# An attention and FFN block on one core: prelude re-ordered, a cast one slot later, eight banks for the last outputs, maxima 8 slots ahead instead of 10

## What is computed

```python
xn = layernorm(X)
Q, K, V = xn @ W_q.T, xn @ W_k.T, xn @ W_v.T          # 16 heads of 16
Qr, Kr = rope(Q), rope(K)
scores = einsum('bhqd,bhkd->bhqk', Qr, Kr) * 16 ** -0.5  # causal
heads = einsum('bhqk,bhkd->bhqd', softmax(scores), V)
attn = heads.reshape(b, t, d) @ W_o.T
ffn = fake_quant_fp8(xn) @ fake_quant_fp8(weight).T + bias   # one scale per tensor
out = X + attn + ffn
```

## Time and profile before

| | us |
|---|---|
| median of 3 runs | 456.89 |
| range of the runs | 455.64 to 457.11 |
| the profiled execution | 456.14 |
| its span in the trace | 454.2 |

### The profile page before, as it was taken

The page is one execution under the profiler, slowest core; times in us unless marked ns, Lnnn a source line. Parts: engine busy times, 40 slices in busy tenths (PEclk is TensorE's granted clock), DMA queues, the critical chain, the costliest instruction groups (busy, mean ns, idle before and its releaser), DMA issues.

```text
span 454.2 us, 9406 instructions
## 1 busy us (share of the span) xinstructions
PE 400.0 (88%) x2911; PEld 234.7 (52%) x2911; DVE 353.9 (78%) x1372; ACT 278.6 (61%) x505; POOL 284.4 (63%) x284
## 2 busy tenths in 40 slices
PE   7906769987889999999999999999999999899866
PEld 7505434443545645564556555655556555464434
DVE  2996778999797978987898869887988698779213
ACT  2664757565763766576756676576667666667631
POOL 2675674468577678667866866778668764245740
PEclk9966898999999999999999999999999999999999
DMA  8859226633267058714762366525762477020111
GB/s 273 270 162 218 39 71 156 132 65 118 84 126 141 2 164 193 136 25 137 198 138 45 116 184 123 92 74 176 138 129 71 149 156 143 2 93 3 49 46 46
DMA packets 34049, 53.16 MB, mean 117 GB/s; under 512 B 4496, under 2 KB 30480, under 8 KB 31120
## 3 DMA queue, kind: packets, MB, share of 16 engines
q1 hardware_dynamic: 34000, 52.57, 46.9%
HBM read 35.52 MB, written 16.78 MB: 115 GB/s over the span
## 4 chain that ended last, share of the span: by engine, by line
PE 45%; DVE 18%; issue 12%; POOL 9%; ACT 9%; DMA 5%; SPq 1%; POOLq 0%; DVEq 0%; ACTq 0%
PE o_ps L931 10%; PE st_ps L844 9%; DVE scratch L600 8%; PE s_ps L864 7%; PE m_ps L829 6%; ACT prob L712 5%; PE m_ps L896 4%; PE m_ps L873 4%; POOL rot L308 3%; POOL rot L300 2%; POOL rot L301 2%; DMA xnT<-x_dram 2%; DMA q_st<-shift 1%; POOL parts L313 1%; POOL prob L458 1%
## 5 line engine op out<-in xcount | busy, mean ns | idle before, releaser
L600 DVE CUSTOM_DVE_ANT_0 scratch<-s_ps,causal 128x512 bf16<-128x512 f32 (+3 forms) x512 | 220.5, 484 | 48.3 <-PE s_ps L864 48.1
L712 ACT ACTIVATE prob<-st_ps 128x512 f32<-128x512 f32 x320 | 174.5, 600 | 103.5 <-PE st_ps L844 102.4
L458 POOL TENSOR_SCALAR_AFFINE_SELECT prob<-prob 128x512 f32<-128x512 f32 (+1 forms) x160 | 92.1, 579 | 127.3 <-ACT prob L712 126.6
L864 PE MATMUL s_ps<-k_st,q_st 96*128 96x512 bf16 (+3 forms) x512 | 122.3, 301 | 24.1 <-DMA k_st<-qk_parts 14.5
L844 PE MATMUL st_ps<-q_st,k_st 98*128 98x128 bf16 (+3 forms) x512 | 122.5, 302 | 15.1 <-ACT prob L712 11.2
L844 PEld LDWEIGHTS st_ps<-q_st,k_st 98*128 98x128 bf16 x512 | 41.2, 97 | 97.5 <-ACT prob L712 57.9
L931 PE MATMUL o_ps<-prob,v_sb 128*17 128x512 f32 (+3 forms) x1024 | 81.4, 435 | 2.3 <-POOL prob L458 1.8
L864 PEld LDWEIGHTS s_ps<-k_st,q_st 96*128 96x128 bf16 x512 | 48.5, 98 | 47.9 <-DVE rowmax L600 17.4
L600 DVE DVE_READ_ACCUMULATOR2_ANT rowmax<- 128x1 f32 x512 | 41.2, 80 | 0.0
L931 PEld LDWEIGHTS o_ps<-prob,v_sb 128*17 128x17 f32 x1024 | 23.0, 96 | 31.0 <-issue 24.4
L313 POOL TENSOR_TENSOR parts<-rot,parts 128x1024 bf16<-128x1024 f32 (+1 forms) x16 | 32.7, 2046 | 2.3 <-ACT parts L698 2.3
(11 more groups left out here) (101 smaller groups left out, 519.1 us busy)
## 6 DMA issues: line engine op xcount, KB each, us to landing
qk_parts<-parts SPq DMA_DIRECT2D x16, 768.0 KB, 3.7
q_st<-qk_parts SPq DMA_DIRECT2D x15, 384.0 KB, 4.9
k_st<-qk_parts SPq DMA_DIRECT2D x15, 384.0 KB, 7.2
xnT<-x_dram SPq DMA_DIRECT2D x8, 512.0 KB, 8.8
q_st<-qk_parts SPq DMA_DIRECT2D x15, 256.0 KB, 3.8
k_st<-qk_parts SPq DMA_DIRECT2D x15, 256.0 KB, 8.3
x_res<-x_dram SPq DMA_DIRECT2D x7, 512.0 KB, 3.5
out_dram<-x_res SPq DMA_DIRECT2D x7, 512.0 KB, 2.9
```

The costliest lines, as they stand in the source:

```text
L458: eng.affine_select(out=ap, in_=ap, compare_op=ALU.is_ge, fill=0.0, base=0, pattern=pat, channel_multiplier=-1).then_inc(masked, 1)
L600: eng.tensor_tensor_reduce(scratch[:, at % 3, col:col + w], s_ps[at % 3][:, col:col + w], causal[:, T - w:T], 1.0, NEG, ALU.add, ALU.max, ...
L712: eng.activation(prob[u][:, half * T:(half + 1) * T], st_ps[ST_BANK[2 * s + half]][:, :], ACT.Exp, scale=SCALE).then_inc(exp_done, 1)
L864: mm = eng.matmul(bank[:, col:col + (qb + 1) * P], q_st[0:ROWS, n % 2, h, qb * P:(qb + 1) * P], k_st[0:ROWS, n % 2, h, 0:(qb + 1) * P], st ...
```

## The change

- **Lead.** `LEAD` 10 to 8. The maxima, and with them "mt" of groups 0 and 1 (one slot later), the first slot, and the slots in which batches 3 to 7 are turned, follow. The second item of V comes one slot earlier.
- **Chain.** The offsets are now tables. The `middle` cast of the keys moves from -21 to -20, their write from -19 to -18. Batch 1 has slots of its own (`EARLY`, `EARLY_CHAIN`), some of them after slot 0.
- **Prelude.** Batch 1's x is loaded ahead of cos and sin; both fills of `k_st` come ahead of the second `invert`; DVE does all of batch 0's remainders and lows; the weights' casts come first on ACT, their splits come early on POOL; `statistics` of batches 6 and 7 move into slots -8 and -6; batch 0's parts are written part by part (`write_first`), two writes more for each of queries and keys; the dummy products go from 26 and 8 to 22 and 6, and 46 new ones fill PE's wait, tied to the last low cast and to the last write.
- **End.** For the last batch "o", "at" and "fin" leave the schedule. Behind it four banks take the turned heads and the outputs, four others the turned `attn`, with four buffers for its copy. The products of the input go in ahead of those of attention. In slot 160 the attention products of blocks 1 and 3 wait for four masks only, and block 2 alone waits for the fifth.

The core of the diff:

```diff
-LEAD = 10
+LEAD = 8
-OFFSETS = {("v", 0): 0, ("mt", 1): 1, ("v", 1): 2, ("o", 0): 23, ("o", 1): 24, ("o", 2): 25, ("o", 3): 26, ("mt", 2): 7,
+OFFSETS = {("v", 0): 0, ("v", 1): 1, ("mt", 1): 2, ("o", 0): 23, ("o", 1): 24, ("o", 2): 25, ("o", 3): 26, ("mt", 2): 7,
            ("at", 0): 28, ("qk", 0): -32, ("at", 1): 29, ("qk", 1): -30, ("fin", 0): 31, ("at", 2): 32, ("mt", 3): 12,
-           ("qk", 2): -27, ("fin", 1): 34, ("at", 3): 34, ("qk", 3): -25, ("fin", 2): 36, ("mt", 0): -4, ("fin", 3): 38}
+           ("qk", 2): -27, ("fin", 1): 34, ("at", 3): 34, ("qk", 3): -25, ("fin", 2): 36, ("mt", 0): -3, ("fin", 3): 38}
-TURN_SLOT = {3: -10, 4: -9, 5: -7, 6: -5, 7: -3}
+EARLY = {("qk", 0): -6, ("qk", 1): -5, ("qk", 2): -4, ("qk", 3): -3}
+CHAIN = {("rotate", 0): -29, ("high", 0): -28, ("remainder", 0): -27, ("middle", 0): -26, ("low", 0): -25,
+         ("write", 0): -24, ("rotate", 1): -24, ("high", 1): -23, ("remainder", 1): -22, ("middle", 1): -20,
+         ("low", 1): -19, ("write", 1): -18, ("read", 0, 0): -18, ("read", 0, 1): -16, ("read", 1, 0): -12,
+         ("read", 1, 1): -11}
+EARLY_CHAIN = {("rotate", 0): -4, ("high", 0): -4, ("remainder", 0): -3, ("middle", 0): -3, ("low", 0): -2,
+               ("write", 0): -1, ("rotate", 1): -1, ("high", 1): -1, ("remainder", 1): 0, ("middle", 1): 2,
+               ("low", 1): 3, ("write", 1): 4, ("read", 0, 0): -1, ("read", 0, 1): 6, ("read", 1, 0): 8,
+               ("read", 1, 1): 9}
+TURN_SLOT = {3: -LEAD, 4: -LEAD + 1, 5: -LEAD + 2, 6: -LEAD + 4, 7: -LEAD + 6}
...
+            def write_first(w):
+                for t, (done, out_) in enumerate(((hi_done, early_out), (mid_done, early_out), (low_done, parts_out))):
+                    eng.wait_ge(done[w], 2)
+                    eng.dma_start(qk_dram[0, w].rearrange("t r j h n -> (j h) t r n")[:, t],
+                                  parts[:, w, t]).then_inc(out_[w], 16)
...
-            for n in range(4):
+            for n in range(3):
                 statistics(n)
-            eng.wait_ge(w_qk_in, 16 * 4)
+            eng.wait_ge(cos_in, 16 * 2)
             rope(0, 0, first_ps[0])
             rope(0, 1, first_ps[1])
             rotate(eng, 0, 0)
             rope(0, 2, first_ps[2])
+            remainder(eng, 0, 0)
             rope(0, 3, first_ps[3])
             rotate(eng, 0, 1)
+            low(eng, 0, 0)
             remainder(eng, 0, 1)
             low(eng, 0, 1)
-            for n in range(4, NB):
+            for n in range(3, 6):
                 statistics(n)
...
-            keep_busy(26)
+            keep_busy(22)
             turn_rows(0)
-            keep_busy(8)
+            keep_busy(6)
             for k in range(4):
                 project_whole(k)
             turn_rows(1)
             turn_rows(2)
+            keep_busy(20)
+            eng.wait_ge(low_done[1], 2)
+            keep_busy(16)
+            eng.wait_ge(parts_out[1], 16)
+            keep_busy(10)
...
+            last = NB - 1
+            eng.wait_ge(max_done, ITEMS * NB)
+            eng.wait_ge(fin_done, 4 * last)
+            for qb in range(NQ):
+                turn_heads(last, qb, tail_o[qb]).then_inc(full["o"], 1)
+            eng.wait_ge(exp_done, HALVES * NB)
+            for qb in range(NQ):
+                turn_attn(last, qb, tail_at[qb]).then_inc(full["at"], 1)
+                if qb > 0:
+                    output_of_attn(last, qb - 1, tail_o[qb - 1], False).then_inc(full["fin"], 1)
+                output_of_input(last, qb, tail_o[qb], True)
+            output_of_attn(last, NQ - 1, tail_o[NQ - 1], False).then_inc(full["fin"], 1)
```

More of the change, by code:

```diff
@@ L214, in attention_ffn_block @@
         first_ps = m_ps + s_ps[0:2]
+        tail_o, tail_at = s_ps + m_ps[0:1], m_ps[1:2] + st_ps + [o_ps]
         turn_ps = (st_ps[0], o_ps)
@@ L223, in attention_ffn_block @@
         parts_out = [sem(f"parts_out{w}") for w in range(2)]
+        early_out = [sem(f"early_out{w}") for w in range(2)]
         first_in = [sem(f"first_in{g}") for g in range(2)]
@@ L461, in _ @@
             nw = NC * D
-            for n in range(3):
-                invert(n)
-            eng.wait_ge(ln_rstd, 6)
+            eng.wait_ge(consts, 6)
             fill_ones(0)
             eng.wait_ge(consts, 7)
-            remainder(eng, 0, 0)
-            low(eng, 0, 0)
+            invert(0)
+            eng.wait_ge(ln_rstd, 2)
+            fill_ones(1)
+            eng.wait_ge(consts, 8)
+            invert(1)
+            eng.wait_ge(ln_rstd, 4)
             split_weights(0)
+            eng.wait_ge(w_split, 1)
+            invert(2)
+            eng.wait_ge(ln_rstd, 6)
             split_weights(1)
+            eng.wait_ge(w_split, 2)
+            eng.memset(v_sb[:, :, :, :], 1.0).then_inc(consts, 1)
+            eng.wait_ge(consts, 9)
+            eng.wait_ge(low_done[1], 2)
+            invert(3)
+            invert(4)
             split_x(1)
-            for n in range(3, 6):
-                invert(n)
-            eng.memset(v_sb[:, :, :, :], 1.0).then_inc(consts, 1)
-            eng.wait_ge(consts, 8)
+            invert(5)
             for slot in range(FIRST_SLOT, END_SLOT):
@@ L658, in _ @@
                     row_max(n, 2 * s + 1)
+                if slot in (-LEAD, -LEAD + 2):
+                    statistics({-LEAD: 6, -LEAD + 2: 7}[slot])
                 if slot in range(1, 2 * NB, 2):
@@ L671, in _ @@
                        .then_inc(qc_done, 1)
+            for qb in range(NQ):
+                norm(NB - 1, qb, tail_o[qb])
+            for qb in range(NQ):
+                finish(NB - 1, qb, tail_o[qb])
         @block.scalar
@@ L735, in _ @@
             normalise(0)
+            eng.wait_ge(w_qk_in, 16 * 2)
+            for parts_of, raw in zip(w_parts, (wq_sb, wk_sb)):
+                eng.copy(parts_of[:, 0], raw).then_inc(w_high, 1)
             copy_turned(0)
@@ L788, in _ @@
                         copy_heads(n, g)
-                for off, step, w in ((-28, high, 0), (-26, middle, 0), (-23, high, 1), (-21, middle, 1)):
-                    n = batch_at(slot, off, 1)
+                for name, step, w in (("high", high, 0), ("middle", middle, 0), ("high", high, 1), ("middle", middle, 1)):
+                    n = chain_at(slot, name, w)
                     if n is not None:
                         step(n, w)
+            for qb in range(NQ):
+                copy_at(NB - 1, qb, tail_at[qb])
         @block.tensor
```

121 lines of the change are left out of this document (76 added, 45 removed).

## The result

The changed kernel takes 460.54 us (median of 8 runs, 459.67 to 463.02), the kernel before 457.0 on the same chip (8 runs, 453.6 to 458.12): ratio 1.0098, 95% interval 1.0062 to 1.0134. The forecast was 442.8 with a range of 439.0 to 449.0. The profiled run of the change took 459.71, its span is 458.0 against 454.2.

The account below looks back on a forecast made before the run. PE was taken to bound the middle batches and DVE batch 0. Prelude -8.5, middle -3.3, shifts +1.4, last-batch maxima +1.0 and end -4.7 sum to -14.1, from 456.89 to 442.8 us; range 439 to 449.

Parts of the forecast that it names:

- The path to the first slot, -3.0: Prelude: last low cast 1.7 us and keys' write 1.3 us sooner, so PE's maxima start at 35.2 instead of 38.21.
- The rule by which more transfers would cost 4 us: Prelude writes in thirds: at about 2.0 us fixed cost each, two more starts add 4 us, sum -10.1; a rival.
- The slots ahead of batch 0, -7.7: Eight slots before batch 0: first exponential at 59.8 instead of 67.54, a gain of 7.7 us lasting until slot 20.
- In batch 0 DVE is the bound and covers both: Batch 0: no cost there from later shifts of groups 0 and 1, because DVE bounds that batch.
- The check by parts (3.0, 3.5 and 1.0): First exponential's 7.7 us gain: 3.0 from the start, 3.5 from the `k_st` fill, 1.0 from the cast ahead of it.
- The clock term of 0.8: PE's clock of 0.8 from 68 to 79 us, after the late exponential, improves; 0.8 us taken between 0 and 2.3.
- The middle, -3.3: Batches 1 to 6: later cast removes a 0.71 us wait each, 4.3; earlier V projection loses 0.15 each time.
- The shifts, +1.4: Shorter lead makes group 0's shifts for slot 20 late by 0.2 us in each of 7 batches.
- The shifts come late in every batch: Rival, 8%: group 0's shifts 1.0 us late per batch instead of 0.2, giving 448.4 us.
- Slower: Rival, 3%: shift landings of 4.6 us make groups 0 and 1 late, 3.5 us in 7 batches, giving 466.
- Two slots of maxima in the last batch, +1.0: Two slots' worth of maxima products move into the last batch's second half, partly covered by PE's waits; costs 1.0 us.
- the end, -4.7: After the last batch: `heads` copy 1.0 us sooner, turns without a reader between; last finish begins 446.9 instead of 451.55.

Follow-up runs that it names:

- run 5: Changed kernel with one number back: SP issues the keys' write in slot -19 instead of -18, all other lists unchanged; 448.85 us, ratio 0.9854.
- run 4: Kernel before with only the keys' middle cast, low cast and write a slot later (-20, -19, -18); 448.44 us, ratio 0.9831.
- run 9: Run 5 with the second V projection back in slot 2, behind the turn of group 1's maxima; 446.34 us, ratio 0.9811.
- run 11: Kernel before with the new end alone; lead, prelude and casts as before; 451.43 us, ratio 0.9912.
- run 12: Kernel before with the late cast and the new end together, old prelude and lead of 10; 444.46 us, ratio 0.9757.
- run 7: Changed kernel with lead 9, batch 1's chain mended and group 1's turn in slot 1 (443.22 us), keys' write put back from -19 to -18; 442.37 us.
- run 6: Run 4 with the second V projection moved to slot 1 and the turn of group 1's maxima to slot 2; 472.09 us, ratio 1.0352.
- run 8: Changed kernel with the shift pairs issued from ACT's queue instead of SP's, SP keeping its wait for the shift; 521.45 us, ratio 1.1442.

## Why the forecast failed, step by step

Two steps failed: the shifts of group 2 behind the late write (11.7 us), and what the earlier start is worth (some 3.5 us). With the write's one number mended (run 5) the time is 448.85, still 6 us above the 442.8. In the spans, run 5 against the kernel before: 5.0 gained ahead of the first landmark where 8.5 were forecast, 1.4 in the middle where 1.9 were, 3.4 behind it where 3.7 were. (Its trace is of its fastest execution: the spans differ by 9.8, the medians on its chip by 6.7.)

**The path to the first slot, -3.0: right.** PE's first maxima came 4.1 us sooner than in the trace before. That trace has a late start: the old prelude's first maxima lie between 37.02 and 38.21 in four traces, the new one's between 33.97 and 34.58 in all, so some 3 us are the change's. The rule by which more transfers would cost 4 us did not decide. By the Trainium skill, DMA: Bandwidth & Descriptors (Rules for kernel authors), the sum was to be -10.1, an estimate; no such loss at the start shows in the rows.

**The slots ahead of batch 0, -7.7: right in the row, wrong in what it is worth.** The first exponential came 6.7 sooner, at 60.87 against the forecast 59.8. The step that failed is "As DVE waits only at the start of batch 0, a gain there lasts until slot 20". The landmark in slot 23 gained 3.4 of it (5.0 in run 5). DVE is the bound of batch 0, so its list had to be summed, not the way to ACT's first exponential. Its first maxima come 3.8 to 4.8 us sooner (35.51 against 39.34 to 40.33 with the old prelude) and have 4.2 us of `statistics` behind them that stood ahead before; and it waits for PE's scores for 8.8 us between 55 and 118, where it waited 3.9 before, as PE stands for the shifts of groups 0 and 2 (1.92 at 57.40, 2.66 at 81.82). "In batch 0 DVE is the bound and covers both" is wrong for the same reason: DVE's maxima need PE's products, and these stand behind the stalled scores on PE. The check by parts (3.0, 3.5 and 1.0) was mis-sized too: the cast alone is worth over 3 of it (run 4), not 1.0. The clock term of 0.8 has no run of its own; ahead of the first landmark the clock rose from 0.90 to 0.96, but behind the two waits just named it was near 0.86 (57 to 69 us and 80 to 92 us), so part of it was lost again.

**The middle, -3.3: right about the cast, and too small.** The 0.71 waits are gone, and run 4 has the cast by itself: 7.5 us. In its trace 5.4 lie between the landmarks, where 4.3 were forecast, and 2.6 ahead of the first, some of which is the earlier start of that trace. The V projection in slot 1 was to cost 0.15 a batch; it brings a new wait of 0.35 for `v_sb`, and a batch 0.27 longer (runs 5 and 9).

**The shifts, +1.4: this is the step that failed.** It looked at group 0's pair, and dismissed the others with "Group 1 moves a slot too, with 1 us in hand." That hand was counted for the scores in slot 5. It was not asked what stands behind that wait in SP's list: the keys' write, then the key reads, then group 2's pair. The cost there is 11.7 us (run 5 against the change); group 2's pair lands after 4.3 to 4.9 instead of 1.8, PE's waits for shifts are 15.3 instead of 7.0, and 3 us more go to the slower clock behind the longest of them. The sign that was named for being wrong, a period of 47.4 or more with `st_ps` waiting for shifts, is the one that came. The rivals "The shifts come late in every batch" (8%) and "Slower" (3%) had the right kind of wait, "Slower" with a landing of 4.6 us as well, but at groups 0 and 1; it happened at group 2, and with a cause that neither had. The chance of 0.95 for faster was unfounded: it rested on five terms, and the list of SP, which the change reorders, was read for group 0's pair alone. The bounds listed for the range (0.5, 0.8, 2, 1.4 and 1) add up to 5.7, where the text goes 3.7 and 3.8 either way.

**Two slots of maxima in the last batch, +1.0, and the end, -4.7: right in sum.** Together -3.7, and the piece behind the last landmark is 3.4 shorter. The last finish is 8.2 us behind the `heads` copy, not 7.5. The end alone gives -4.1 in the old kernel (run 11).

**What reaches the forecast time.** The late cast and the end give -11.5 together (run 12); the new prelude at a lead of 10 adds nothing to be told; a lead of 9 gives 443.2. So 442.8 was within reach with other table entries, but by other terms than the forecast's: more from the cast, next to nothing from the prelude.

## What to carry to other kernels

Where a wait moves one step later in an in-order queue, list everything that stands behind it in that queue and follow it to the end: here a 4 KB transfer's wait held a 768 KB write, this held the reads, and these slowed the next 4 KB transfer. A slot number in a table fixes an order, not a time; the late write is harmless alone (runs 4 and 7), and with a later turn in front of it the middle lost 12 to 18 us (the change against run 5, run 6 against run 4), so price pairs that meet on one queue. And take a gain at the start from the list of the engine that bounds the next stage: time in which that engine had other work to do was not idle.

## What the runs showed of the hardware

A transfer of 4 KB landed in 1.6 to 1.8 us when nothing was under way (217.74 in the change), in 3.0 to 3.4 when it was issued 0.4 us behind a write of 768 KB (218.78 in the kernel before), and in 4.3 to 5.5 when it was issued 4.3 us behind key reads of 768 KB in three pieces (the change, run 6). With 7.2 and 7.3 us between them it took 1.8 and 2.3 (runs 5 and 4). Reads right behind it on its own queue cost it nothing; reads beside it on another queue did (run 8).

PE's clock fell to 0.50 of full speed behind waits of 1.90 and 3.63 us (the two rows in the section on the result), and did not fall behind one of 1.7 us.

DVE was held by POOL once more in the new prelude: `ve`, 128x4, which takes 0.17 us, took 1.84 while POOL ran a subtraction of two operands (from 33.14 for 2.36 us). In the changed kernel:

```profile
31.58 0.17 DVE L574 TENSOR_SCALAR ve<-mv_b 128x4 f32<-128x4 f32 x1
33.69 1.84 DVE L574 TENSOR_SCALAR ve<-mv_b 128x4 f32<-128x4 f32 x1
```

It ends with POOL's instruction, at 35.5. The Trainium skill, SBUF — State Buffer (Who interferes with whom), has the two engines share ports under an exclusive lock; this row agrees, and it is part of why DVE's first maxima came at 35.5 while PE's products had started at 34.07.
